# Attention and a routed expert layer on one core: GpSimd sums the marks of the chosen experts, and eight steps of the first part stand at other places

## What is computed

```python
xn = _layernorm(x, axis=-1)
# attention
qkv = einsum('bsd,ed->bse', xn, Wqkv_w) + Wqkv_b
scores = einsum('bqhd,bkd->bhqk', q, k) * scale        # causal mask, then softmax
ctx = einsum('bhqk,bkd->bqhd', attn, v)
attn_out = einsum('bsd,ed->bse', ctx, out_w) + out_b
# experts
probs = softmax(einsum('td,ed->te', xt, w_router))
top_w, top_e = top_k(probs, 4);  top_w = top_w / sum(abs(top_w))
for e in range(16):
    coeff = sum(where(top_e == e, top_w, 0.0), axis=-1)
    h = silu(xt @ w_gate[e]) * (xt @ w_up[e])
    out = out + coeff[:, None] * (h @ w_down[e])
return x + attn_out + out
```

## Time and profile before

| what | value |
|---|---|
| runs shown | 439.45, 440.17, 440.76 us; median 440.17 |
| the profiled execution's own time | 438.48 us |
| its span, first to last instruction | 436.7 us |
| mean granted clock of TensorE, share of full speed | 0.959 |
| PE busy | 390.2 us (89%) |
| POOL busy | 301.6 us (69%) |
| DVE busy | 230.8 us (53%) |
| ACT busy | 216.9 us (50%) |

### The profile page before, as it was taken

The page is one execution under the profiler, slowest core; times in us unless marked ns, Lnnn a source line. Parts: engine busy times, 40 slices in busy tenths (PEclk is TensorE's granted clock), DMA queues, the critical chain, the costliest instruction groups (busy, mean ns, idle before and its releaser), DMA issues.

```text
span 436.7 us, 8048 instructions
## 1 busy us (share of the span) xinstructions
PE 390.2 (89%) x2553; PEld 310.5 (71%) x2553; DVE 230.8 (53%) x588; ACT 216.9 (50%) x362; POOL 301.6 (69%) x327
## 2 busy tenths in 40 slices
PE   7979879999999988579999999999999999999900
PEld 6535545555555544369999999999999999999800
DVE  5767899998888742124444444444444444434400
ACT  4645354567676667225444545445544455444300
POOL 7864046329999585735888888888888888888530
PEclk9989998999999999869999999999999999999965
DMA  7699447568873988723545554464454554554035
GB/s 232 184 273 286 118 144 185 164 167 183 201 180 100 311 255 295 231 68 63 79 69 79 77 80 72 68 88 73 77 79 73 76 80 77 77 75 61 2 73 120
DMA packets 53145, 56.69 MB, mean 130 GB/s; under 512 B 10720, under 2 KB 48272, under 8 KB 52848
## 3 DMA queue, kind: packets, MB, share of 16 engines
q0 software_dynamic: 15440, 21.51, 29.2%
q1 hardware_dynamic: 24848, 22.06, 19.3%
q10 hardware_dynamic: 12816, 12.60, 9.8%
HBM read 36.87 MB, written 23.07 MB: 137 GB/s over the span
## 4 chain that ended last, share of the span: by engine, by line
PE 61%; POOL 11%; DVE 8%; DMA 4%; issue 3%; another core or an unknown queue 3%; SPq 2%; ACT 2%; POOLq 0%; ACTq 0%; DVEq 0%
PE bank L842 31%; PE bank L851 15%; POOL wgu L581 8%; DVE pmax L1266 4%; PE bank L833 4%; PE bank L687 2%; PE bank L777 2%; PE bank L788 2%; PE bank L696 2%; POOL xs L507 1%; DMA qs_wgu<-q_d 1%; DMA out_dram<-pt,slots 1%; POOL ks L516 1%; PE bank L815 1%
## 5 line engine op out<-in xcount | busy, mean ns | idle before, releaser
L1491 DVE COPY late<-bank 128x256 f32<-128x256 f32 x79 | 33.5, 424 | 112.3 <-PE bank L833 92.2
L842 PEld LDWEIGHTS bank<-late,choice 128*128 128x128 f32 x640 | 78.8, 195 | 12.0 <-issue 9.2
L842 PE MATMUL bank<-late,choice 128*128 128x128 f32 x640 | 80.0, 279 | 8.0 <-issue 7.0
L851 PE MATMUL bank<-wdn,late 128*128 x316 | 81.7, 381 | 0.3 <-DVE late L1495 0.2
L1147 ACT ACTIVATE late<-bank 128x256 f32<-128x256 f32 x79 | 30.3, 384 | 100.6 <-PE bank L842 79.3
L612 POOL DMA_INDIRECT out_dram<-pt,slots x40 | 62.9, 1573 | 23.8 <-DMA out_dram<-xs 9.8
L842 PEld LDWEIGHTS bank<-late 128*128 128x128 f32 x624 | 75.4, 192 | 3.5 <-DVE late L1491 1.2
L842 PE MATMUL bank<-late 128*128 128x128 f32 x624 | 76.2, 275 | 0.6 <-DVE late L1491 0.5
L1061 ACT ACTIVATE pt<-bank 128x512 f32<-128x512 f32 x96 | 55.9, 598 | 40.0 <-PE bank L777 38.5
L1266 DVE TRANSPOSE_TENSOR_REDUCE pmax<-bank 128x16 f32<-128x512 f32 x96 | 66.4, 705 | 12.5 <-PE bank L687 10.8
L612 POOL DMA_INDIRECT odd_d<-pt,slots x39 | 61.3, 1572 | 14.0 <-issue 8.9
(11 more groups left out here) (159 smaller groups left out, 514.6 us busy)
## 6 DMA issues: line engine op xcount, KB each, us to landing
qs_late<-q_d SPq DMA_DIRECT2D x20, 256.0 KB, 5.7
q_d<-early SPq DMA_DIRECT2D x16, 256.0 KB, 3.6
wgu<-in_L_ffn_w_gate_dram ACTq DMA_DIRECT2D x8, 512.0 KB
wgu<-in_L_ffn_w_up_dram ACTq DMA_DIRECT2D x8, 512.0 KB
wdn<-in_L_ffn_w_down_dram ACTq DMA_DIRECT2D x8, 512.0 KB
qs_wgu<-q_d SPq DMA_DIRECT2D x12, 256.0 KB, 5.8
xs<-in_L_attn_x_dram SPq DMA_DIRECT2D x4, 512.0 KB, 5.1
xn_d<-early SPq DMA_DIRECT2D x4, 512.0 KB, 5.0
```

Source lines behind the costliest of these rows:

```text
L842: mm = pe.matmul(bank[:, 2 + j % 2, f * P:(f + 1) * P], wst[j % 2][:, c, f * P:(f + 1) * P], xT[:, j % 2, c, :], start=(c == 0), stop=(c = ...
L851: mm = pe.matmul(bank[:, 4 + j % 2, 0:D], hT[:, j % 2, c, :], wdn[:, bass.ds(e * FC + c, 1), :], start=(c == 0), stop=(c == FC - 1))
L1491: dve.tensor_copy(xT[:, j % 2].rearrange("p c t -> p (c t)"), bank[:, 0, 0:D]).then_inc(xgT_ready, 1)
```

## The change

GpSimd takes over the sum of the marks: three additions for each part instead of one reduction on DVE. It stands in POOL's program between the biases of groups 2 and 3 and `copy_k(3)`. DVE's `sum_tops(0)` moves up to step (0, 8), and `mark_choices(1)` from step (0, 11) to (0, 10). PE's count waits for all six additions. In the first part, PE's third group of queries (half 0) and `transpose_vr(1)` stand ahead of the first first-pass block. ACT's `root(2)` stands behind the last tiles of group 1, its `keep_xT(2)` ahead of `keep_kh(1)`, its `keep_vl(1)` ahead of `split_q(2, 0)`. DVE's `measure(3)` stands ahead of `keep_ql(1, 0)`, `keep_kl(1)` and `scale(3)` ahead of the first maximum, and `split_max(0)` ahead of `keep_kl(3)`.

```diff
             pool.wait_ge(xb_ready, NT)
+            join_choices(0)
+            join_choices(1)
             copy_k(3)
...
+            def join_choices(part):
+                ts = slice(CHOICE_PARTS[part][0] * GT, CHOICE_PARTS[part][1] * GT)
+                pool.wait_ge(marked, part + 1)
+                so_far = onehot[:, ts, 0]
+                for k in range(1, TOP_K):
+                    if k > 1:
+                        pool.wait_ge(chosen_ready, (TOP_K - 1) * part + k - 1)
+                    pool.tensor_tensor(chosen[:, ts], so_far, onehot[:, ts, k], ALU.add).then_inc(chosen_ready, 1)
+                    so_far = chosen[:, ts]
...
-                pe.wait_ge(chosen_ready, len(CHOICE_PARTS))
+                pe.wait_ge(chosen_ready, (TOP_K - 1) * len(CHOICE_PARTS))
...
             transpose_x(2)
-            first_scores(0)
+            transpose_vr(1)
             project_q(2, 0)
-            transpose_vr(1)
-            first_scores(1)
+            first_scores(0, 1)
             project_q(2, 1)
...
             split_q(0, 0)
-            root(2)
             normalise(1, 2, 3)
             split_q(0, 1)
             normalise(1, 3, 4)
+            root(2)
             keep_vr(0)
...
             keep_vr(1)
+            keep_xT(2)
             keep_kh(1)
             root(3)
-            keep_xT(2)
+            keep_vl(1)
             split_q(2, 0)
-            keep_vl(1)
...
             keep_kl(0)
+            measure(3)
             keep_ql(1, 0)
-            measure(3)
             keep_xT(2)
             keep_ql(1, 1)
+            keep_kl(1)
+            scale(3)
             first_maxima(0)
-            scale(3)
-            keep_kl(1)
             keep_ql(2, 0)
...
                 if (b, s) == (0, 8):
                     mark_choices(0)
-                if (b, s) == (0, 9):
-                    join_choices(0)
                     sum_tops(0)
-                if (b, s) == (0, 11):
+                if (b, s) == (0, 10):
                     mark_choices(1)
-                if (b, s) == (1, 0):
-                    join_choices(1)
...
             join_max(0)
+            split_max(0)
             keep_kl(3)
-            split_max(0)
```

More of the change, by code:

```diff
@@ L258, in attention_and_experts @@
         cells_ready = sem("cells_ready")
+        marked = sem("marked")
         route_ready = sem("route_ready")
@@ L1242, in mark_choices @@
                 dve.wait_ge(xn_stored[0], 32)
[L1243 to L1251, removed]
+                dve.tensor_tensor(onehot[:, start:stop].rearrange("p t k e -> p (t k) e"),
+                                  top_ef[:, start:stop].rearrange("p t k -> p (t k)").unsqueeze(2).to_broadcast([P, n, E]),
+                                  iota_e[:].unsqueeze(1).to_broadcast([P, n, E]), ALU.is_equal).then_inc(marked, 1)
             def sum_tops(part):
```

## The result

The changed kernel takes 443.84 us (median, 442.81 to 447.05) against 440.50 us for the kernel before (439.45 to 441.90): ratio 1.0107, 95% interval 1.0075 to 1.0139. It is slower, by about 3.3 us; 440.9 was predicted, with 443.0 as the upper end. The profiled execution of the changed kernel took 446.9 us, span 445.2, clock 0.945.

What follows compares the result with a forecast made beforehand. DVE was taken to pace 48.4 to 66.6 us, POOL's marks 97.5 to 139, then PE. Terms -4.0, +0.35, +3.15 and +1.2 gave +0.7 on 440.17: 440.9 us, range 437.4 to 443.0.

Steps and rivals of the forecast that it cites:

- first part: Reordered queries and transposes before block 3: no stop for batch 0's queries, no low clock; block 3 4.0 us earlier.
- split: Splitting the maxima ahead of the keys on DVE: batch 1's maxima start later, a loss of 0.35 us.
- sums behind eight biases: Six additions on POOL after the biases delay PE's count; 3.15 us lost at batch 3's first block.
- clock at the count: PE's stop at the count makes its clock fall: a loss of 1.2 us, bounds 0 and 1.45.
- `scale(3)` 1.05 us: In the first part, DVE's scaling ahead of the last normalised tile, placed at 32.35 us, was to take 1.05 us.
- late queries of batch 1: Rival: full DMA engines deliver batch 1's queries late, PE waits 2 us; sum +2.7, 442.9 us; chance 0.06.
- the fall behind the split: Rival: standing still at block 14 lowers PE's clock, PE paces three or four steps: +1.2, 442.1 us; chance 0.08.
- the long and the cheap additions: Rivals on POOL: additions of 0.65 us, 442.4 us, chance 0.10; of 0.2 us, 438.1, 0.22 including an earlier POOL start.
- some 2.8 us: Expected length of PE's stop at the count, from about 75.6 to 78.4 us, waiting for POOL's additions.
- the four query matmuls of an earlier low stretch: First-part queries after the 2.26 us stop: 3.33 us instead of 1.88; their 1.45 was the count's upper clock bound.

Runs made afterwards that it cites:

- f1: The kernel before with no edit, run again for a second profile on the slower chip: 441.29 us, ratio 0.9989.
- g1: Changed kernel with sums on DVE as before, keys ahead of the split, POOL's key copies held back until the last tiles are scaled: 421.43 us, ratio 0.9970.
- g4: Changed kernel with sums on DVE as before and keys ahead of the split, POOL's key copies not held back: 422.13 us, ratio 0.9989.
- e1: Changed kernel with DVE summing the marks at its old steps; only first part and split in new order: 423.27 us, ratio 1.0008.
- f3: Changed kernel with additions, key copies and second weights ahead of the biases on POOL, and keep_kl(3) ahead of split_max(0): 438.50 us, ratio 0.9925.
- f4: Changed kernel with additions, key copies, second weights ahead of biases, keys ahead of split, POOL's earlier key copies held back until DVE's scaling: 436.71 us, ratio 0.9880.
- g2: Kernel before, old first part, with the sums on POOL ahead of the biases of groups 2 and 3: 422.13 us, ratio 0.9988.
- e3: Changed kernel with the additions, batch 3's key copies and second weights ahead of the biases of groups 2 and 3 on POOL: 422.99 us, ratio 1.0000.
- e2: Kernel before with the additions on POOL and the new routing steps, first part in the old order: 427.05 us, ratio 1.0099.
- e4: Changed kernel with keep_kl(3) ahead of split_max(0) again: 426.46 us, ratio 1.0081.
- f2: The changed kernel with no edit, run again for a second profile on the slower chip: 444.94 us, ratio 1.0061.
- The filled stop: Changed kernel with 26 identity matmuls into an unused bank on PE ahead of its wait at the count: 430.87 us, ratio 1.0190.

## Why the prediction was wrong

The profiles give one account. From block 3 to the cast in us, by where the sums stand and by which comes first on DVE, the keys of group 3 (`keep_kl(3)`) or the split of the maxima:

```
sums on DVE                keys first   60.81 to 60.83  before, f1, g1, g4
                           split first  61.91           e1
on POOL, ahead of biases   keys first   59.84 to 59.87  f3, f4, g2
                           split first  60.94           e3
on POOL, behind biases     keys first   63.67           e2 (clock stays up)
                           keys first   65.21           e4 (clock falls)
                           split first  67.35, 67.60    changed, f2
```

So each term of the sum has a measured value, on the profiled executions. The last term is what the others leave:

| term | predicted | measured | from |
|---|---|---|---|
| first part | -4.0 | -3.09 | block 3, 36.65 to 33.56 |
| split | +0.35 | +1.09 | 61.91 less 60.82; 60.94 less 59.86 gives 1.08 |
| sums behind eight biases | +3.15 | +2.85 | 63.67 less 60.82 |
| clock at the count | +1.2 | +2.59 | 67.35 less 61.91 less 2.85 |
| sum | +0.7 | +3.44 | the cast, 97.47 to 100.91 |

**First part: right in mechanism, 0.9 us too large.** The queries came without a stop and at full clock, as said. The step that failed is "`scale(3)` 1.05 us": it took 2.46, because the new order puts it beside POOL's copies, and ACT's last tile waited for it. The pair g1 and g4 shows this by one wait: 1.12 us at block 3. The trace of before had it already: there `scale(2)`, at 19.17 us beside POOL's copies, took 2.1 us, and I took the quiet `scale(3)` as the price. What was gained at block 3 was passed on whole: g4 has the same 60.8 us from there to the cast as before, so no late queries of batch 1. The gain also depends on something outside the kernel's text. It was 4.12 us on the chip of the f kernels (37.68 to 33.56), but where the load came in time, in the run with the sums alone, the old first part had block 3 at 33.86 by itself. That leaves 0.3 us, less than the 1.09 us that the split costs, which would explain why e1 gained nothing. It is not shown: the kernel before was not profiled on that chip, and in g2, with the old first part on the same chip, the load came 1.84 us late.

**Split: the wait was right, the fall of the clock was not in the forecast.** DVE waits 0.42 us and PE 1.23, as predicted (0.45 and 1.2). I had costed only DVE's wait and put the fall behind the split at 8 in 100, as a rival of +1.2. It came in every profile with the split first (0.62 to 0.75 from 47.0 to 51.5 us), and in none with the keys first (1.00). The maxima start 0.51 us later than in g4, whose first part is the same (46.97 to 47.48), and the first nine take 6.14 us instead of 5.67.

**Sums: right.** Six additions took 2.76 us, 2.8 predicted, and the long and the cheap additions are both out. The estimate from the Trainium skill (GPSIMD Engine Reference, section 3.1), 2.1 us, was too low: each took 0.42 to 0.46 us, where its table scaled by size gives 0.28. `weigh_choices(0)` came 1.68 us earlier relative to the marks than before (1.64 predicted). The count came 3.46 us later, by e4 against g4 from block 3 (41.44 and 37.98 us); 3.45 was predicted. Less of it reached the cast, 2.85. The stop was 3.80 us instead of some 2.8: counted from block 3, PE came to the count 0.2 us earlier than the forecast has it, and the sixth addition let it go 0.8 us later, about what the split cost beyond its term (0.74).

**Clock at the count: right in kind, half the size.** This is the largest miss, 1.4 us, and this is the step that failed: I had taken the four query matmuls of an earlier low stretch (1.45 us lost) as the most that such a fall can cost. Here the low stretch lasts from the count to about 82 us and holds the blocks for which DVE waited 6.14 us, so it delays a chain that goes through both engines. The filled stop gives nearly the same value by another way: 24.80 less 22.24 is 2.56 us. In e4 the clock was back sooner (0.50 from 76 to 78 us, 0.92 from 78 to 80) and cost only 1.54 (65.21 less 63.67). Why it came back sooner there is open, and so is the share of the order of the split: with the sums behind the biases and a fall in both, split first costs 2.14 us (67.35 less 65.21) and not 1.09.

**How it adds up.** 0.91 + 0.74 + 1.39 less 0.30 is 2.74, the distance from +0.7 to +3.44. The medians are 3.34 apart. Three misses of one sign carried the result past the upper end. The clock is in two of them, and the range took in a fall at the count at 1.45 us at most. The rest of the profiled execution, 5.1 us behind the cast, is not the change's: the kernel before has the same stops at other lengths, and the first chip has no long one. What releases PE there stays open.

## What to carry to other kernels

When work is moved to an engine that has slack on average, what counts is what stands ahead of it in that engine's program and who waits for it: the same six additions cost 4.4 us behind eight biases and gained 1 us ahead of them, together with the key copies and weights that moved with them. Cost a stop of PE as the stop and the low clock behind it, and if another engine waits for what runs in that stretch, take the whole stretch and not the few matmuls in it. And when an operation is moved, look at which engine works beside it at its new place.

## What the hardware showed that I had not expected

- DVE's four operations on 128x4 f32 between and behind the reciprocals took 0.35 to 0.63 us beside POOL's copies from f32 to fp32r and 0.16 to 0.17 us without them, in two kernels that differ only in when the copies start. The reciprocals kept their 0.18 us. The Trainium skill says (GPSIMD Engine Reference, section 8, Key points) that GpSimd shares its SBUF interfaces with VectorE and that DVE instructions with two SBUF inputs or in a 2-port mode meet contention. The rows with two tensor inputs agree, with a factor of two to four. The TENSOR_SCALAR row, 0.54 us instead of 0.17, has one; whether it ran in such a mode the profile does not show.
- The length of a stop of PE alone did not tell whether the clock falls. Stops of 2.26 us (before) and 1.23 us (changed, at the split) were followed by stretches at 0.50 and 0.59 of full clock; one of 2.42 us at the count (e2) was followed by full clock. Two stops of the same length at the same place differ too. In e2 the granted clock is 0.50 from 64 to 66 us, in e4 it stays at 1.00; the L801 and L800 rows are the same eight matmuls:

```profile
62.28 0.47 PE L700 MATMUL bank<-qs_late,ks 96*128 96x512 f32 x1 [1.65 <-DVE pmax L1273]
...
64.81 1.94 PE L801 MATMUL bank<-pt,v_all 128*32 128x512 f32 x8
```

```profile
62.00 0.48 PE L700 MATMUL bank<-qs_late,ks 96*128 96x512 f32 x1 [1.65 <-DVE pmax L1272]
...
64.11 1.06 PE L800 MATMUL bank<-pt,v_all 128*32 128x512 f32 x8
```

- The kernel before takes 423 us on one chip and 441 on another. Much of it is a stop of PE at the start of the experts' tiles, 7.9 to 10.7 us in the four profiles of the slower chip and none on the faster. PE's row names DVE's copy (L1491, in the changed kernel L1493) or nothing. DVE waits there itself, for something that the profile calls only "remote"; in f1:

```profile
193.09 0.42 DVE L1491 COPY late<-bank 128x256 f32<-128x256 f32 x1 [11.68 <-remote]
```
